# Half of the first tile's pairs among fields 0 to 15 taken ahead in two steps of 32 samples, and the first store held

## The chip, the core and the metric

The kernel runs on one core of a Trainium2 chip. TensorE does matmuls (its weight loads are rows of their own, PEld), VectorE (DVE) elementwise work and reductions, ScalarE (ACT) activations and copies, GpSimd (POOL) issues the indirect gathers, SyncE (SP) the other DMA transfers. The time is that of one execution on the device in microseconds, the median of several runs.

## What is computed

A recommender tower for 1024 samples, 33 fields and vectors of 128 numbers. The reference, cut to what matters:

```python
e = stack([tbl_f[ids[:, f]] for f in range(33)], axis=1)      # (1024, 33, 128)
row, col = np.triu_indices(33, k=1)                            # 528 pairs
inner = e[:, row] * e[:, col]
fm = relu(einsum('bpd,ad->bpa', inner, attn_W) + attn_b)
scores = einsum('ba,bpa->bp', gnn_feature, fm)
attn = softmax(scores, axis=1)
attn_output = einsum('bp,bpd->bd', attn, inner) * 100.0
z = concatenate([gnn_feature, attn_output, gnn_feature], axis=1)
h = relu(z @ W_top1 + b_top1); h = relu(h @ W_top2 + b_top2)
y = h @ W_top3
```

## The kernel before

**Tiles and steps.** The samples go in T = 8 tiles of 128. A tile has STEPS = 32 steps of GROUPS = 4 samples, so there are ALL = 256 steps S. The 528 pairs of a sample are laid out as K = 16 distances by F = 33 fields: pair (f, f + k) modulo 33 with k = 1 to 16. To read them without a modulus, x is held transposed in `xt` (128 rows for the vector's numbers, then sample, then 33 fields and fields 0 to 15 once more, written by `repeat`). A step has COLS = 4 x 528 = 2112 columns.

**One step.** VectorE multiplies (`product`, L418) into one of 4 buffers of `products`. ScalarE rounds most columns to the faster fp32r type (`round_inner`, L316, `inner_hi`), VectorE subtracts to get the rest (`rest_of_inner`, L423, `low_parts`). TensorE's `hidden` (L571) takes the columns in 5 chunks of 416 or 424: a *native* chunk is one fp32 matmul (L580, two records in the profile), a *split* chunk three fp32r matmuls (L587, L588, L589). `NATIVE[S]` says how many chunks are native: 4 and 3 in steps 0 and 1, 2 in six steps of a tile, 1 in the others. Two chunks share a buffer of the PSUM ring of 3; ScalarE's `relu` (L308) empties a buffer into `fm` (3 buffers). After hidden(S) of an even step, `reduce_steps(S - 2)` (L610) makes the scores of two steps: each step has 8 matmuls of 264 columns, whose 32 weight columns come from `gnn_blocks` at a place of their own for each group of samples j, and which write 32 rows of PSUM each (rows 32j on), so that the four j use different quarters of the array.

**Around the steps.** TensorE also transposes x (`transpose_x`, L620, eight fields at a time, into the ring; ScalarE's `evacuate_xt`, L347, copies them to `xt`), at steps 18, 20, 22, 24 and 26 for the next tile, and does `fields` (L634) and `mlp` for the tile before. Softmax parts stand at the first steps of a tile. `units` lists everything that takes a buffer of the ring, in the order in which TensorE claims them.

**The first tile.** GpSimd gathers 33 fields into `x_rows`, one indirect transfer a field (L280). TensorE transposes all five groups of fields as they land, then starts hidden(0). VectorE's product(0) waits for all five groups and the repeated fields.

**Queues.** Every engine runs its list in order. SyncE: loads of inputs, then `store_rows(0)` (the 128 x 33 rows of `x_rows` to `x_dram`, L230, when all fields are gathered), `store_rows(1)`, then the loads of `x_fields` from `x_dram` (L219) for the first tile. GpSimd's gather of tile 1 waits for the first store (it overwrites `x_rows`) and, group by group, for the transposes of tile 0. Gather 2 waits for the second store in the same way.

Of the kernel before, what the change touches and what calls it, by code (L numbers as in the profile page):

```python
# [7 lines left out]
ALU = mybir.AluOpType  # L8
# [4 lines left out]
def afm_tower(nc, gnn, ids, tables, w1, b1, w2, b2, w3, attn_w, attn_b, out):  # L13
    P = 128
    B, D = gnn.shape
    F = len(tables)
# [13 lines left out]
    assert EDGES[0][-1] == EDGES[1][-1] == COLS and ALL % 2 == 0  # L30
    H1, H2 = w1.shape[1], w2.shape[1]
# [13 lines left out]
    NATIVE[0], NATIVE[1] = 4, 3  # L45
    FIRST = 0
    SPLIT = COLS - min(EDGES[S % 2][NATIVE[S]] for S in range(ALL))
# [4 lines left out]
    XT_AT = (18, 20, 22, 24, 26)  # L52
    MLP_AT = (19, 21, 23)
    MAX_AT, EXP_AT, INV_AT, SCALE_AT, TURN_AT = 1, 2, 2, 3, 4
# [10 lines left out]
    def jobs_of(S):  # L65
# [4 lines left out]
        if s in XT_AT and t + 1 < T:  # L70
            jobs.append(("x_t", t + 1, XT_AT.index(s)))
# [7 lines left out]
    units = [("x_t", 0, c) for c in range(XJ)]  # L79
    for S in range(ALL):  # L80
        pair, odd = divmod(S, 2)
        units += [("hidden", pair, j) for j in ((3, 4) if odd else (0, 1, 2))] + jobs_of(S)
# [4 lines left out]
    with ctx:  # L87
# [96 lines left out]
        def taken_out(unit):  # L184

            kind, a, b = unit
            if kind == "hidden":
                return s_fm, SLOTS * a + b + 1
# [13 lines left out]
        def native_cols(S):  # L202
            return EDGES[S % 2][NATIVE[S]]

        def chunk_place(S, c):

            pair, odd = divmod(S, 2)
            j, h = divmod(CHUNKS * odd + c, 2)
            return slot(("hidden", pair, j)), h
# [4 lines left out]
        def _(sp):  # L214
# [26 lines left out]
            sp.dma_start(b2_sb[:], b2.rearrange("(m p) -> p m", p=P), allow_slow_non_contiguous=True).then_inc(s_weights, 16)  # L241
            store_rows(0)
# [52 lines left out]
        def _(act):  # L295
            def relu(pair, j):
                act.wait_ge(s_hidden, 2 * (SLOTS * pair + j + 1))
                S = 2 * pair
                if j == 0 and S >= FM_BUFS:
                    act.wait_ge(s_red, (S - FM_BUFS) // 2 + 1)  # L300
                if j == 2 and S + 1 >= FM_BUFS:
                    act.wait_ge(s_red, (S + 1 - FM_BUFS) // 2 + 1)
                n = THIN if j == 2 else WIDE
                at = [(S + c // CHUNKS) % FM_BUFS * COLS + EDGES[c // CHUNKS][c % CHUNKS] for c in (2 * j, 2 * j + 1)]
                first = fm[:, 0, 0:1]
                dst = bass.AP(tensor=first.tensor, offset=first.offset + at[0],
                              ap=[first.ap[0], [at[1] - at[0], 2], [1, n]])
                nc.scalar.activation(dst, slot(("hidden", pair, j))[:, :, 0:n], ACT.Relu,  # L308
                                     bias=attn_b_sb[:, 0:1]).then_inc(s_fm, 1)

            def round_inner(S):
                act.wait_ge(s_inner, S + 1)
                if S >= HI_BUFS:
                    act.wait_ge(s_hidden, CHUNKS * (S - HI_BUFS + 1))
                at = native_cols(S)
                nc.scalar.copy(inner_hi[:, S % HI_BUFS, 0:COLS - at], plain[:, S % INNER_BUFS, at:]).then_inc(s_hi, 1)  # L316
# [52 lines left out]
            for c in range(XJ):  # L369
                evacuate_xt(0, c)  # L370
                if c < K // FU:
                    repeat(0, c)
            round_inner(0)
            round_inner(1)
            for S in range(ALL):
                t, s = divmod(S, STEPS)
                relu(S // 2, 2 if S % 2 else 0)
                if part_at(S, EXP_AT) is not None:
                    exps(part_at(S, EXP_AT))
                if S + 2 < ALL:  # L380
# [3 lines left out]
                relu(S // 2, 3 if S % 2 else 1)  # L384
                if S % 2:
                    relu(S // 2, 4)
# [5 lines left out]
                if t + 1 < T and s - 1 in XT_AT[0:K // FU]:  # L392
# [13 lines left out]
        def _(dve):  # L406
            def product(S):
                if S >= INNER_BUFS:
                    dve.wait_ge(s_hidden, CHUNKS * (S - INNER_BUFS + 1))
                t, s = divmod(S, STEPS)  # L410
# [311 lines left out]
```

## Time and profile before

| | us |
|---|---|
| median of 3 runs | 1270.39 (1270.38 to 1270.89) |
| the profiled execution | 1270.63 |
| its span, first to last instruction | 1268.2 |
| TensorE busy | 1201.0 (95%) |
| VectorE busy | 1147.9 (91%) |
| ScalarE busy | 1018.7 (80%) |
| GpSimd busy | 451.8 (36%) |

The profile lists instructions with their start and duration, groups them by line and shape, names for an engine's idle time the releaser of the instruction that ended it, and gives the work of each engine in any stretch. Two instructions of an engine can overlap a little, so the distance of two starts is a better price than a duration. Matmul ends are modelled; a matmul's real cost is the distance to the next one's start. A row with "x8" is eight instructions in a row with their summed time.

### The profile page before, as it was taken

What the parts mean: (1) busy time and instruction counts of PE and PEld (TensorE: products, weight loads), DVE (VectorE), ACT (ScalarE), POOL (GpSimd) and SP (SyncE); (2) the same over time, 40 slices, a digit from 0 to 9 for tenths busy, and PEclk for the clock granted to TensorE, in tenths of its full rate; (3) what the DMA queues carried; (4) which work ended last, traced back from release to release, by engine and by line L of the source; (5) the groups of instructions that cost most, each with busy time, mean ns of one, the idle gap of its engine ahead of it and who ended that gap; (6) DMA issues with size and microseconds to landing.
All of it is one profiled execution on the core that took longest, in us unless ns stands there. A gap on an engine that the chain in (4) does not pass through costs nothing.

```text
span 1268.2 us, 20736 instructions
## 1 busy us (share of the span) xinstructions
PE 1201.0 (95%) x8732; PEld 898.7 (71%) x8732; DVE 1147.9 (91%) x649; ACT 1018.7 (80%) x1039; POOL 451.8 (36%) x270
## 2 busy tenths in 40 slices
PE   1499999999999999999999999999999999999998
PEld 1267676777777777777777777677777777777766
DVE  2399899998999989999899989999799998999994
ACT  1288898778987889878897798978888788887883
POOL 6587684018800386005840088201880000000000
PEclk9999999999999999999999999999999999999999
DMA  4211410311103111131101311031110300011001
GB/s 108 97 34 50 105 32 26 102 45 30 34 13 125 31 32 28 30 106 37 32 20 47 106 27 32 20 111 39 30 34 21 117 18 1 1 29 39 17 9 38
DMA packets 54859, 58.83 MB, mean 46 GB/s; under 512 B 10728, under 2 KB 49136, under 8 KB 53744
## 3 DMA queue, kind: packets, MB, share of 16 engines
q1 hardware_dynamic: 46304, 40.20, 10.4%
q0 software_dynamic: 8448, 17.32, 5.2%
q8 instruction: 69, 1.13, 0.4%
q14 instruction: 22, 0.18, 0.0%
q10 hardware_dynamic: 16, 0.00, 0.0%
HBM read 36.12 MB, written 17.31 MB: 42 GB/s over the span
## 4 chain that ended last, share of the span: by engine, by line
PE 83%; ACT 8%; issue 4%; DVE 2%; POOL 2%; another core or an unknown queue 1%; DMA 1%; SPq 0%; ACTq 0%; DVEq 0%; POOLq 0%
PE scores L610 19%; PE ring L580 17%; PE ring L587 13%; PE ring L589 12%; PE ring L588 12%; PE ring L634 4%; ACT fm L308 3%; ACT inner_hi L316 3%; PE ring L620 2%; POOL x_rows L280 2%; PE ring L654 1%; DVE products L418 1%; ACT exp_pairs L323 1%; PE ring L648 1%
## 5 line engine op out<-in xcount | busy, mean ns | idle before, releaser
L308 ACT ACTIVATE fm<-ring,attn_b_sb 128x848 f32<-128x848 f32 (+1 forms) x640 | 597.2, 971 | 183.1 <-PE ring L580 174.3
L418 DVE TENSOR_TENSOR products<-xt 128x2112 f32<-128x2112 f32 x256 | 601.9, 2351 | 37.1 <-ACT xt L347 37.1
L280 POOL DMA_INDIRECT x_rows<-in_tbl,ids_all x264 | 451.1, 1709 | 498.2 <-PE ring L620 408.3
L423 DVE TENSOR_TENSOR low_parts<-products,inner_hi 128x1688 fp32r<-128x1688 f32 (+4 forms) x256 | 467.1, 1825 | 57.1 <-ACT inner_hi L316 56.0
L587 PE MATMUL ring<-inner_hi,attn_wt_lo 128*128 128x424 f32 (+1 forms) x971 | 433.1, 446 | 5.1 <-ACT fm L308 5.1
L316 ACT CAST inner_hi<-products 128x1688 fp32r<-128x1688 f32 (+4 forms) x256 | 392.3, 1532 | 5.2 <-DVE products L418 5.2
L589 PE MATMUL ring<-inner_hi,attn_wt_hi 128*128 128x424 f32 (+1 forms) x971 | 344.1, 354 | 0.0
L588 PE MATMUL ring<-low_parts,attn_wt_hi 128*128 128x424 f32 (+1 forms) x971 | 343.7, 354 | 0.0
L580 PE MATMUL ring<-products,attn_wt 128*128 128x424 f32 (+1 forms) x618 | 275.8, 542 | 10.0 <-issue 6.4
L610 PE MATMUL scores<-fm,gnn_blocks 128*32 128x264 f32 x4096 | 254.6, 389 | 6.5 <-ACT exp_pairs L323 6.4
L587 PEld LDWEIGHTS ring<-inner_hi,attn_wt_lo 128*128 128x128 f32 x971 | 182.6, 188 | 70.8 <-issue 37.6
L588 PEld LDWEIGHTS ring<-low_parts,attn_wt_hi 128*128 128x128 f32 x971 | 183.0, 188 | 43.5 <-issue 40.1
L610 PEld LDWEIGHTS scores<-fm,gnn_blocks 128*32 128x32 f32 x4096 | 120.0, 109 | 107.7 <-issue 13.8
L589 PEld LDWEIGHTS ring<-inner_hi,attn_wt_hi 128*128 128x128 f32 x971 | 182.4, 188 | 5.2
L580 PEld LDWEIGHTS ring<-products,attn_wt 128*128 128x128 f32 x618 | 104.6, 190 | 85.4 <-issue 78.2
L620 PE MATMUL ring<-ident,x_rows 128*128 128x128 f32 x264 | 39.2, 292 | 34.0 <-DMA x_rows<-in_tbl,ids_all 31.1
L634 PE MATMUL ring<-attn_t,x_fields 128*128 128x128 f32 x512 | 62.5, 275 | 2.0 <-ACT attn_t L401 1.4
L634 PEld LDWEIGHTS ring<-attn_t,x_fields 128*128 128x128 f32 x512 | 61.8, 191 | 3.2 <-issue 3.1
L347 ACT COPY xt<-ring 128x1024 f32<-128x1024 f32 (+1 forms) x40 | 38.5, 964 | 31.3 <-PE ring L620 15.7
L620 PEld LDWEIGHTS ring<-ident,x_rows 128*128 128x128 f32 x264 | 33.0, 151 | 39.4 <-DMA x_rows<-in_tbl,ids_all 25.7
L473 DVE TENSOR_TENSOR attn<-ring,xt 128x1024 f32<-128x1024 f32 x30 | 36.6, 1220 | 2.8 <-PE ring L634 2.8
L481 DVE TENSOR_REDUCE pooled<-attn 128x32 f32<-128x1024 f32 x30 | 36.5, 1216 | 0.1
(53 smaller groups left out, 203.9 us busy)
## 6 DMA issues: line engine op xcount, KB each, us to landing
x_dram<-x_rows SPq DMA_DIRECT2D x8, 2112.0 KB, 6.6
x_fields<-x_dram SPq DMA_DIRECT2D x128, 128.0 KB
x_rows<-in_tbl,ids_all POOLq DMA_INDIRECT x264
attn_t<-attn_turned SPq DMA_DIRECT2D x124, 32.0 KB, 1.9
w_sb<-in_W_top SPq DMA_DIRECT2D x2, 512.0 KB
x_fields<-in_r_gnn_feature SPq DMA_DIRECT2D x1, 512.0 KB
h<-in_W_top SPq DMA_DIRECT2D x1, 256.0 KB
ids_all<-in_ids SPq DMA_DIRECT2D x1, 132.0 KB, 2.7
```

Of the source, the lines that this page charges most:

```text
L280: nc.gpsimd.indirect_dma_start(out=x_rows[:, f, :], out_offset=None, in_=tables[f], in_offset=bass.IndirectOffsetOnAxis(ap=ids_all[:, t, f ...
L308: nc.scalar.activation(dst, slot(("hidden", pair, j))[:, :, 0:n], ACT.Relu, bias=attn_b_sb[:, 0:1]).then_inc(s_fm, 1)
L316: nc.scalar.copy(inner_hi[:, S % HI_BUFS, 0:COLS - at], plain[:, S % INNER_BUFS, at:]).then_inc(s_hi, 1)
L418: nc.vector.tensor_tensor(dst, a, b, ALU.mult).then_inc(s_inner, 1)
L423: nc.vector.tensor_tensor(inner[:, S % INNER_BUFS, at:end], plain[:, S % INNER_BUFS, at:end], inner_hi[:, S % HI_BUFS, 0:end - at].bitcast ...
L580: nc.tensor.matmul(dst, attn_wt[:], plain[:, S % INNER_BUFS, begin:end], start=True, stop=True)\
L587: nc.tensor.matmul(dst, attn_wt_lo[:], hi, start=True, stop=False)
L588: nc.tensor.matmul(dst, attn_wt_hi[:], lo, start=False, stop=False)
L589: nc.tensor.matmul(dst, attn_wt_hi[:], hi, start=False, stop=True).then_inc(s_hidden, 1)
L610: last = nc.tensor.matmul(scores[I * j:I * j + I, h, 0:HALF], block_of(s, j), fm[:, S % FM_BUFS, at:at + HALF], start=s == 0, stop=s == ST ...
L620: last = nc.tensor.transpose(to[:, n // 4, n % 4 * P:(n % 4 + 1) * P], x_rows[:, FU * c + n, :], ident[:])
L634: last = nc.tensor.matmul(bank[:, h, to:to + QS * I], x[:, n, :], own[:, :, n, :], start=True, stop=True)
```

## The change

1. **Two steps ahead.** Steps S = -2 and -1 are added. Each takes 32 samples and the pairs (f, f + k) with f = 0 to 7 and k = 1 to 8, which need fields 0 to 15 alone: 64 pairs a sample, 2048 columns a step, 4 chunks of 512, all native. They stand after the first two transposes; the transposes of groups 2, 3 and 4 follow them.
2. **Short steps.** Steps 0 to 15 (the same 64 samples) have 464 pairs left a sample: 1856 columns, 4 chunks of 464. `product` makes them in two instructions (distances 1 to 8 with fields 8 to 32, and distances 9 to 16 with all fields). NATIVE[0], NATIVE[1] become 3, 2.
3. **Scores.** `reduce_steps(-2)`, after hidden(0), makes the scores of the samples ahead: 64 matmuls of 64 columns, each writing 8 runs of 8 columns in the scores' 33-column rows. In the short steps the first half of a sample's scores has 200 columns (8 runs of 25) instead of 264.
4. **The first store** waits until hidden(1) is done (QUIET = 2), and with it all that stands behind it on SyncE.
5. Chunks are numbered through the program and paired in that order (`CHUNK_LIST`, `PAIR_OF`), so a relu of a short step has 2 x 464 columns, of a step ahead 2 x 512. The two `repeat` copies of the first tile come after the relus of the steps ahead.

```diff
+    AHEAD, AHEAD_SAMPLES = 8, 32
+    BEGIN = -2
+    SHORT = -BEGIN * AHEAD_SAMPLES // GROUPS
-    NATIVE[0], NATIVE[1] = 4, 3
+    NATIVE[0], NATIVE[1] = 3, 2
...
+    def edges(S):
+        if S < 0:
+            return list(range(0, AHEAD_SAMPLES * AHEAD_PAIRS + 1, 512))
+        if S < SHORT:
+            return list(range(0, LEFT + 1, LEFT // 4))
+        return EDGES[S % 2]
...
+        if S == -1:
+            jobs += [("x_t", 0, c) for c in range(2, XJ)]
...
+            sp.wait_ge(s_hidden, hidden_by(QUIET - 1))
             store_rows(0)
             store_rows(1)
...
+                if S < 0:
+                    pieces = [((S - BEGIN) * AHEAD_SAMPLES, AHEAD_SAMPLES, 0, AHEAD, 1, AHEAD)]
+                elif S < SHORT:
+                    pieces = [(GROUPS * S, GROUPS, AHEAD, F - AHEAD, 1, AHEAD), (GROUPS * S, GROUPS, 0, F, AHEAD + 1, K - AHEAD)]
+                else:
+                    pieces = [(GROUPS * (S % STEPS), GROUPS, 0, F, 1, K)]
...
+            dve.wait_ge(s_xt_out, 2)
+            product(-2)
+            product(-1)
             dve.wait_ge(s_xt_out, XJ)
             dve.wait_ge(s_repeat, K // FU)
             product(0)
...
+                if S < 0:
+                    for i in range(AHEAD_SAMPLES):
+                        step, j = divmod((S - BEGIN) * AHEAD_SAMPLES + i, GROUPS)
+                        columns = fm[:, S % FM_BUFS, i * AHEAD_PAIRS:(i + 1) * AHEAD_PAIRS]
+                        yield step, j, step == 0, near[j][:, :, 0:AHEAD], columns.rearrange("p (k f) -> p k f", f=AHEAD)
+                    return
...
+                        if S < SHORT and h == 0:
+                            columns = fm[:, S % FM_BUFS, j * NEAR:(j + 1) * NEAR]
+                            yield s, j, False, near[j][:, :, AHEAD:F], columns.rearrange("p (k f) -> p k f", f=F - AHEAD)
+                            continue
...
-            for c in range(XJ):
+            for c in range(2):
                 transpose_x(0, c)
             pe.wait_ge(s_zero, 3)
-            for S in range(ALL):
+            for S in range(BEGIN, ALL):
                 hidden(S)
...
-                if S >= 2 and S % 2 == 0:
+                if S >= BEGIN + 2 and S % 2 == 0:
                     reduce_steps(S - 2)
```

**TensorE at the start, before.** L620 are the transposes (33 fields), L580 a native chunk, L587 to L589 a split one.

```order
3 L620 MATMUL ring<-ident,x_rows 128x128 x33
4 L580 MATMUL ring<-products,attn_wt 128x424 x4
5 L587 MATMUL ring<-inner_hi,attn_wt_lo 128x416
6 L588 MATMUL ring<-low_parts,attn_wt_hi 128x416
7 L589 MATMUL ring<-inner_hi,attn_wt_hi 128x416
8 L580 MATMUL ring<-products,attn_wt 128x416
```

**TensorE at the start, now.** The same lines are L682, L627 and L634 to L636; L673 are scores.

```order
3 L682 MATMUL ring<-ident,x_rows 128x128 x16
4 L627 MATMUL ring<-products,attn_wt 128x512 x8
5 L682 MATMUL ring<-ident,x_rows 128x128 x17
6 L627 MATMUL ring<-products,attn_wt 128x464 x3
7 L634 MATMUL ring<-inner_hi,attn_wt_lo 128x464
8 L635 MATMUL ring<-low_parts,attn_wt_hi 128x464
9 L636 MATMUL ring<-inner_hi,attn_wt_hi 128x464
10 L673 MATMUL scores<-fm,gnn_blocks 32x8x8 x64
11 L627 MATMUL ring<-products,attn_wt 128x464 x2
```

Eight chunks of 512 stand between the transposes of 16 and of 17 fields, and 64 matmuls of scores between hidden(0) and hidden(1).

**VectorE, the first products and subtractions, before** (L418 and L423).

```order
10 L418 TENSOR_TENSOR products<-xt 128x2112 x2
11 L423 TENSOR_TENSOR low_parts<-products,inner_hi 128x416
12 L418 TENSOR_TENSOR products<-xt 128x2112
13 L423 TENSOR_TENSOR low_parts<-products,inner_hi 128x848
14 L418 TENSOR_TENSOR products<-xt 128x2112
15 L423 TENSOR_TENSOR low_parts<-products,inner_hi 128x1264
```

**VectorE at the same place, now** (L464 and L470).

```order
10 L464 TENSOR_TENSOR products<-xt 128x2048 x2
11 L464 TENSOR_TENSOR products<-xt 128x800
12 L464 TENSOR_TENSOR products<-xt 128x1056
13 L464 TENSOR_TENSOR products<-xt 128x800
14 L464 TENSOR_TENSOR products<-xt 128x1056
15 L470 TENSOR_TENSOR low_parts<-products,inner_hi 128x464
16 L464 TENSOR_TENSOR products<-xt 128x800
17 L464 TENSOR_TENSOR products<-xt 128x1056
18 L470 TENSOR_TENSOR low_parts<-products,inner_hi 128x928
```

Two products of 2048 columns come first, and each later product is now two instructions with 1856 columns in all.

## Rows read from the trace of the kernel before

**Rows 1.** The page, part 1: busy us, share of the span, instructions.

```profile
PE 1201.0 (95%) x8732; PEld 898.7 (71%) x8732; DVE 1147.9 (91%) x649; ACT 1018.7 (80%) x1039; POOL 451.8 (36%) x270
```

**Rows 2.** Stretches, columns as the first line says, busy in us.

```profile
core 0: us, PE busy (x) PEld busy (x) DVE busy (x) ACT busy (x) POOL busy (x), PEclk, DMA share, GB/s
15.00:46.00 31.00, 5.88 (x24) 4.70 (x24) 0.23 (x2) 5.49 (x5) 23.43 (x25) 1.00 0.20 52
46.00:54.70 8.70, 2.18 (x9) 1.78 (x9) 2.41 (x2) 1.37 (x3) 0.07 (x1) 1.00 0.62 256
...
60.30:133.20 72.90, 72.56 (x502) 52.62 (x501) 72.61 (x38) 64.23 (x64) 53.34 (x32) 1.00 0.22 65
203.00:353.00 150.00, 147.96 (x1089) 111.02 (x1088) 142.18 (x82) 126.87 (x130) 64.10 (x35) 1.00 0.17 48
```

**Rows 3.** Timeline of the head: start us, us, engine, line, instructions, [idle before].

```profile
35.99 1.97 PE L620 MATMUL ring<-ident,x_rows 128*128 128x128 f32 x8 [7.95 <-DMA x_rows<-in_tbl,ids_all]
46.19 2.18 PE L620 MATMUL ring<-ident,x_rows 128*128 128x128 f32 x9 [8.22 <-DMA x_rows<-in_tbl,ids_all]
...
47.43 0.34 SPq L230 DMA_DIRECT2D x_dram<-x_rows  x1
...
38.00 1.08 ACT L347 COPY xt<-ring 128x1024 f32<-128x1024 f32 x1 [7.68 <-PE ring L620]
50.91 1.35 ACT L347 COPY xt<-ring 128x1024 f32<-128x1024 f32 x2 [11.83 <-remote]
...
52.29 4.63 DVE L418 TENSOR_TENSOR products<-xt 128x2112 f32<-128x2112 f32 x2 [37.07 <-ACT xt L347]
...
54.75 1.75 PE L580 MATMUL ring<-products,attn_wt 128*128 128x424 f32 x2 [6.38 <-issue]
```

**Rows 4.** The chain of waits in plain steps, TensorE: start us, us.

```profile
65.93 0.19 PE ring L588
...
67.46 1.92 PE scores L610 x32
...
72.59 0.71 PE ring L580 x2
```

**Rows 5.** Timeline of VectorE from 56 us.

```profile
56.84 0.58 DVE L423 TENSOR_TENSOR low_parts<-products,inner_hi 128x416 fp32r<-128x416 f32 x1
57.34 2.35 DVE L418 TENSOR_TENSOR products<-xt 128x2112 f32<-128x2112 f32 x1
...
66.48 1.92 DVE L423 TENSOR_TENSOR low_parts<-products,inner_hi 128x1696 fp32r<-128x1696 f32 x1
```

**Rows 6.** Timeline at the clock's rise, weight loads and a matmul row.

```profile
58.42 0.33 PEld L580 LDWEIGHTS ring<-products,attn_wt 128*128 128x128 f32 x1 [0.37 <-issue]
59.00 0.19 PEld L580 LDWEIGHTS ring<-products,attn_wt 128*128 128x128 f32 x1 [0.25 <-issue]
...
60.28 1.22 PE L580 MATMUL ring<-products,attn_wt 128*128 128x416 f32 x3
```

**Rows 7.** L610 alone in 0.03 us, columns as in rows 2.

```profile
67.41:67.44 0.03, 0.03 (x4) 0.03 (x8) 1.00 0.00 0
```

**Rows 8.** The page, part 5, weight loads of the scores.

```profile
L610 PEld LDWEIGHTS scores<-fm,gnn_blocks 128*32 128x32 f32 x4096 | 120.0, 109 | 107.7 <-issue 13.8
```

**Rows 9.** Timelines of GpSimd, SyncE and TensorE around the second gather.

```profile
54.63 3.11 POOL L280 DMA_INDIRECT x_rows<-in_tbl,ids_all  x1 [8.88 <-DMA x_dram<-x_rows]
...
124.70 0.33 SPq L230 DMA_DIRECT2D x_dram<-x_rows  x1
...
133.20 1.03 PE L620 MATMUL ring<-ident,x_rows 128*128 128x128 f32 x8
...
153.81 1.06 PE L620 MATMUL ring<-ident,x_rows 128*128 128x128 f32 x8 [0.76 <-ACT fm L308]
...
172.20 0.27 PE L620 MATMUL ring<-ident,x_rows 128*128 128x128 f32 x1
```

**Rows 10.** Timeline of TensorE, fields of the first tile.

```profile
241.86 1.95 PE L634 MATMUL ring<-attn_t,x_fields 128*128 128x128 f32 x16
```

More of the change, by code:

```diff
@@ L76, in jobs_of, with hidden_by, relus_by, pairs_of_steps @@
         return jobs
-    units = [("x_t", 0, c) for c in range(XJ)]
-    for S in range(ALL):
-        pair, odd = divmod(S, 2)
-        units += [("hidden", pair, j) for j in ((3, 4) if odd else (0, 1, 2))] + jobs_of(S)
+    CHUNK_LIST = [(S, c) for S in range(BEGIN, ALL) for c in range(chunks(S))]
+    CHUNK_NO = {chunk: n for n, chunk in enumerate(CHUNK_LIST)}
+    PAIR_OF = [CHUNK_LIST[n:n + 2] for n in range(0, len(CHUNK_LIST), 2)]
+    def hidden_by(S):
+        return CHUNK_NO[S, chunks(S) - 1] + 1
+    def relus_by(S):
+        return CHUNK_NO[S, chunks(S) - 1] // 2 + 1
+    def pairs_of_steps(S):
+        return (S - BEGIN) // 2
+    units = [("x_t", 0, c) for c in range(2)]
+    for S in range(BEGIN, ALL):
+        units += [("hidden", n, 0) for n, pair in enumerate(PAIR_OF) if pair[0][0] == S] + jobs_of(S)
     units += [("fields", T - 1, c) for c in (2, 3)] + [("mlp", T - 1, n) for n in range(3)]
@@ L202, in native_cols @@
         def native_cols(S):
[L203 removed]
+            return edges(S)[NATIVE[S]] if S >= 0 else edges(S)[-1]
         def chunk_place(S, c):
[L207 to L209 removed]
+            return divmod(CHUNK_NO[S, c], 2)
         block = ctx.enter_context(nc.Block())
@@ L368, in _ @@
             nc.scalar.copy(attn_wt_hi[:], attn_wt[:]).then_inc(s_setup, 1)
-            for c in range(XJ):
+            for c in range(2):
                 evacuate_xt(0, c)
[L371 to L375, printed above, removed]
+            for S in range(BEGIN, ALL):
                 t, s = divmod(S, STEPS)
-                relu(S // 2, 2 if S % 2 else 0)
+                out_now = [n for n, pair in enumerate(PAIR_OF) if pair[1][0] == S]
+                relu(out_now[0])
                 if part_at(S, EXP_AT) is not None:
                     exps(part_at(S, EXP_AT))
-                if S + 2 < ALL:
+                if 2 <= S + 2 < ALL:
                     round_inner(S + 2)
@@ L383, in _ @@
                     scale_attn(part_at(S, SCALE_AT))
-                relu(S // 2, 3 if S % 2 else 1)
-                if S % 2:
-                    relu(S // 2, 4)
+                for n in out_now[1:]:
+                    relu(n)
+                if S in FIRST_REPEAT_AT:
+                    repeat(0, FIRST_REPEAT_AT[S])
                 for kind, of, c in jobs_of(S):
@@ L526, in _ @@
             product(0)
-            product(1)
-            rest_of_inner(0)
-            product(2)
-            for S in range(ALL):
+            for S in range(BEGIN, ALL):
                 t, s = divmod(S, STEPS)
-                if S + 1 < ALL:
+                if 0 <= S + 1 < ALL:
                     rest_of_inner(S + 1)
@@ L571, in hidden @@
             def hidden(S):
-                pe.wait_ge(s_inner, S + 1)
-                for c in range(CHUNKS):
-                    begin, end = EDGES[S % 2][c:c + 2]
-                    bank, h = chunk_place(S, c)
-                    dst = bank[:, h, 0:end - begin]
+                pe.wait_ge(s_inner, S - BEGIN + 1)
+                for c in range(chunks(S)):
+                    begin, end = edges(S)[c:c + 2]
+                    n, h = chunk_place(S, c)
+                    dst = slot(("hidden", n, 0))[:, h, 0:end - begin]
                     if h == 0:
-                        claim(("hidden", S // 2, (CHUNKS * (S % 2) + c) // 2))
-                    if c < NATIVE[S]:
+                        claim(("hidden", n, 0))
+                    if S < 0 or c < NATIVE[S]:
                         nc.tensor.matmul(dst, attn_wt[:], plain[:, S % INNER_BUFS, begin:end], start=True, stop=True)\
```

104 lines of the change are left out of this document (59 added, 45 removed).

## The prediction

> **What bounds the kernel now.** I read the busy shares first and then the table of stretches, which says where the busy share is not the whole story. TensorE is busy for 95% of the span [rows 1]. By stretches [rows 2] the kernel has a head of 54.7 us, in whose last two parts TensorE works 5.88 us of 31 and 2.18 of 8.7, and after it a body in which it is busy all the time: 72.56 of 72.90 us in the first 18 steps, 147.96 of 150 us in one later tile. So there are two ways to save: start the body earlier, or take matmul time out of the body. The change tries both: it does 4096 columns of hidden products in the head, where TensorE is idle.
>
> The head, in order of time [rows 3]: TensorE transposes the third group of eight fields at 35.99, as soon as its gather lands, and ScalarE copies it out at 38.00, 2.0 us later; the two groups before it stand in the same way. The fourth group is transposed at 46.19 and copied at 50.91, 4.72 us later, so 2.7 us behind the pattern, and the profile can only name "remote" for it. Meanwhile SyncE issued the 2 MB store of x_rows at 47.43, and the DMA engines moved 256 GB/s in that stretch against 52 before it [rows 2, 3]. Products follow at 52.29, hidden(0) at 54.75.
>
> In the body's first 18 steps VectorE is as full as TensorE: 72.61 of 72.90 us [rows 2]. Both would have to get faster, so both are summed below. TensorE's chain of waits in a plain step is a row of matmuls with no hole in it [rows 4].
>
> **Units, all at full clock.** In the chain a matmul of a split chunk of 424 columns takes 0.19 us, the three of a chunk 0.58; a native chunk is 0.71 us, in two records; the scores of two steps, 32 records, take 1.92 us [rows 4]. In columns: 464 native is 0.71 x 464/424 = 0.78, 464 split 0.63. VectorE: a subtraction of 416 columns takes 0.58 us, of 1696 columns 1.92, so 1.05 ns a column and 0.14 fixed, of which 0.08 overlaps the next instruction (56.84 + 0.58 against 57.34) [rows 5].
>
> **Start of the body.** If the held store is what delayed the fourth copy, the copy moves from 50.91 to 48.2: 2.7 us. The alternative is zero. I take 2.7, because the copies without a store beside them come after 2.0 us and nothing else is in flight there; it is one case, so a rival below. product(0) has 800 + 1056 columns in two instructions instead of 2112 in one: 0.90 + 1.17 = 2.07 against 2.27, 0.2 us less. hidden(0) thus begins at 54.75 - 2.9 = 51.85. The work taken ahead must be out of the way by 46.19: products of 2048 columns, 2.3 us each, from about 29.2, when the second group's copy ends (its row stands 9.9 us before the third's), eight chunks of 512 from 31.5. At half clock a chunk costs 1.71 us (1.41 for 424, since a record's weight load of 0.33 comes 0.37 after the one before [rows 6]), so 13.7 us and an end at 45.2 if the clock never rose; in this trace it rose about 4.1 us into steady work (54.75 to between 58.42 and 59.00, where the weight load of L580 goes from 0.33 to 0.19 us and the records from 0.70 to 0.35 apart, the levels of 1.2 and 2.4 GHz; the granted clock in the profile's column does not show it) [rows 3, 6]. Then they end near 40.5. Either way they cost nothing; neither do their four relus of some 1.2 us, hidden in the same hole of ScalarE (38.00 + 1.08 to 50.91).
>
> **hidden(0).** Before: 54.75 to 60.28, 5.5 us, of which 4.1 at half clock. After: three native chunks at 1.55 at half clock; 4.1 us cover 2.65 of them, the rest 0.27, the split chunk 0.63: 5.0. Saved 0.5.
>
> **Steps 1 to 18, hidden.** Before there are 26 native and 64 split chunks: 26 x 0.71 + 64 x 0.58 = 55.6 us. After, steps 1 to 15 have 21 native and 39 split chunks of 464 (40.9 us) and steps 16 to 18 are as before (9.2 us): 50.1. Saved 5.5. With eight pairs of scores (15.4) the sum of before is 71.0 of the 72.9 measured from 60.28 to 133.20 [rows 6, 9]; I leave that 1.9 as it is.
>
> **Scores of the short steps.** 32 records go in eight groups of four that run side by side (four matmuls are in the array at once in [rows 7]), 0.24 us a group. In half of the groups 264 columns become 200; if their time goes by columns, 0.058 us less each, 0.23 for a pair of steps, 1.9 for eight.
>
> **Scores of the samples taken ahead.** This is what the change adds to TensorE's full stretch: 64 matmuls of 64 columns, 128 records, between hidden(0) and hidden(1). Three prices. By columns alone a group of four is 0.24 x 64/264 = 0.058 us, 32 groups 1.9 us. By the weight load, which now lasts longer than the matmul that should cover it (109 ns [rows 8]), 32 x 0.109 = 3.5 us. By L610's own rate, 1.92 us for 32 records, 60 ns each, 7.7 us. I take 3.5: eight loads and four matmuls are under way within the same 0.03 us [rows 7], so records can follow each other far closer than 60 ns, and the load is the next thing that is longer than the columns. Both ends stay for the range.
>
> The Trainium skill speaks against me here. "TensorE: Matmul & The Clock Gate", section "Wait — 56ns, not 53.3ns?", says that without hardware decoding the sequencer spends about 62 ns on each matmul, which bounds short ones; 128 of them would be 7.9 us. The trace's 60 ns a record of L610 looks like that rule, but eight loads under way at once do not. The case is a rival, priced from L610's row.
>
> **Is TensorE still the bound?** VectorE's short step is 2.07 + 1.53 (1392 columns) = 3.6, or 3.1 where two chunks are native (928 columns). From 49.6 to the subtraction of step 18 it has 16 short products (33.1), 16 short subtractions (0.6 + 6 x 1.04 + 9 x 1.53 = 20.6), four long products (9.1) and three long subtractions (5.1), 68 us, so it is through near 117.5. TensorE's sum ends hidden(18) at 51.85 + 5.0 + 3.5 + 50.1 + 13.5 + 1.9 = 125.9 against 133.20. ScalarE was busy for 64.23 of the 72.90 us before, and its share of a step shrinks with the same columns. TensorE stays last.
>
> **The held store.** SyncE issues it when hidden(1) is done, 51.85 + 5.0 + 3.5 + 2.8 = 63.2 instead of 47.43. Behind it on SyncE's queue wait the second store and the loads of x_fields, and on GpSimd the whole second gather: its first row moves from 54.63 to 70.4, and the second store, which comes when its last has landed, from 124.70 to 140.5 [rows 9]. The transposes that need the gather come at 133.20 to 172.20, 7 us earlier after; the last group has 24 us left. So the delay costs nothing, but the second store, 7.2 us long like the first (47.43 to 54.63), now runs at 140.5 to 147.7, and the third group of transposes, which read x_rows, moves from 153.81 [rows 9] to 146.5: the edge of it.
>
> **Sum.** 2.7 + 0.2 + 0.5 + 5.5 + 1.9 - 3.5 = 7.3 us. Later steps are as before and shift as a whole. Against the profiled execution (1270.63 us, 1268.2 of it span) that is 1263.3; the median of the runs shown, 1270.39, is 0.2 below it, so I say **1263.1**.
>
> **Rivals.**
> - *The stall stays, or moves to the second store* (18%). For: "remote" names no cause, and the second store meets the transposes of the second tile at its edge. Against: the pattern of 2.0 us. 2.7 less gained: 1265.8.
> - *More than summed* (14%): the array is still at full clock when hidden(0) begins, since it worked from 31.5 on (half of 4.1, 2.05 us more), or the scores ahead cost 1.9. 1261.1 and 1261.5. Against the first: it stands idle from about 41.5 to 46.19 and 47.4 to 51.85.
> - *The short scores keep L610's rate* (10%): 7.7 instead of 3.5, 1267.3. The page's rule would come out there too.
> - *Other gains lost* (5%): the ring of three slots or ScalarE holds up the short steps, or the later steps' waits for relu take the lead back. About 1269.5.
> - *Slower* (3%): the short matmuls do not run four abreast, because each has its own weights and writes eight runs of eight columns. Nearest row: 1.95 us for 16 records of 128 columns that use the whole array [rows 10], 0.12 each, 15.6 us for 128. 12.1 more than I took: 1275.2. It turns slower from 10.8 us on, 84 ns a record.
> - The rest, 50%, is my forecast, within 1261.8 to 1264.5.
>
> That the change does not do what it says can be set aside: the order of instructions shows the eight chunks of 512 ahead of the last transposes.
>
> **Numbers.** Measurements of this kernel can tell about 0.2%, 2.5 us, from no change. Faster: 50 + 18 + 14 and half of the 10 at the limit, 87%. Within: the other half and the 5, 10%. Slower 3%. The range 1260.0 to 1267.6 leaves out some 2% below (both of the extra gains) and the last cases above.
>
> **What would show it.** The fourth copy out of x_t should begin near 48.2, hidden(0) near 51.9; L673, the new line of the scores, should show its first 128 records in 1.9 to 3.5 us (7.7 would be L610's rate, 15.6 the slower rival); the transposes of the second tile should begin at about 125.9, and every later stage 7 us earlier, with the later tile as long as before. Wrong would be: a "remote" wait that is still there, TensorE waiting for relu or for the subtractions in steps 1 to 15, or a stall at 140 to 150.

## The result, and the profile after

The changed kernel takes **1264.38 us** (median of 6 runs, 1263.74 to 1264.97); the kernel before, beside it on the same chip, 1270.6. The ratio is 0.995, with a 95% interval of 0.994 to 0.9961: faster by 6.2 us, half a per cent and clear of the noise, where 7.3 us were forecast. The profiled execution took 1263.74 us, its span 1261.6.

The total is close, but two of the terms behind it are wrong, and their errors cancel in part. The stretches of the new kernel, in the columns of [rows 2] (busy time and instructions of each engine, then TensorE's granted clock, DMA share, GB/s):

```profile
core 0: us, PE busy (x) PEld busy (x) DVE busy (x) ACT busy (x) POOL busy (x), PEclk, DMA share, GB/s
...
46.00:54.77 8.77, 2.18 (x9) 1.78 (x9) 2.21 (x3) 1.93 (x4) 1.83 (x2) 0.50 0.08 22
60.14:62.06 1.92, 1.92 (x129) 1.83 (x128) 1.92 (x3) 1.21 (x2) 0.00 (x0) 1.00 0.03 9
62.06:127.52 65.46, 65.46 (x463) 44.50 (x457) 62.49 (x48) 54.53 (x54) 46.54 (x27) 1.00 0.18 59
202.00:352.00 150.00, 147.97 (x1095) 111.00 (x1087) 142.17 (x80) 126.96 (x130) 75.57 (x43) 1.00 0.18 52
```

The third of these rows is the body's first part: 65.46 us from hidden(1) to the second tile's first transposes, where the kernel before had 72.92 (60.28 to 133.20) [rows 2, 6, 9]. That is 7.46 us less, and 7.4 were summed. The row ahead of it is what the scores of the samples taken ahead add: 1.92 us, not 3.5. A later stretch of 150 us is as full as before [rows 2].

The head is where the surprise is. The timeline of the new kernel's head (start us, us, engine, line, instructions, [idle before <- what ended it]):

```profile
28.44 0.94 POOL L320 DMA_INDIRECT x_rows<-in_tbl,ids_all  x1 [0.30 <-issue]
29.09 4.49 DVE L464 TENSOR_TENSOR products<-xt 128x2048 f32<-128x2048 f32 x2 [13.99 <-issue]
29.69 2.50 POOL L320 DMA_INDIRECT x_rows<-in_tbl,ids_all  x1 [0.31 <-issue]
32.50 1.90 POOL L320 DMA_INDIRECT x_rows<-in_tbl,ids_all  x1 [0.30 <-issue]
34.71 0.95 POOL L320 DMA_INDIRECT x_rows<-in_tbl,ids_all  x1 [0.31 <-issue]
...
40.36 1.04 PE L682 MATMUL ring<-ident,x_rows 128*128 128x128 f32 x8
...
45.48 1.08 ACT L386 COPY xt<-ring 128x1024 f32<-128x1024 f32 x1 [2.79 <-remote]
...
47.19 0.94 POOL L320 DMA_INDIRECT x_rows<-in_tbl,ids_all  x1 [0.31 <-issue]
48.42 2.18 PE L682 MATMUL ring<-ident,x_rows 128*128 128x128 f32 x9 [7.03 <-DMA x_rows<-in_tbl,ids_all]
51.17 1.35 ACT L386 COPY xt<-ring 128x1024 f32<-128x1024 f32 x2 [4.62 <-PE ring L682]
52.56 4.23 DVE L464 TENSOR_TENSOR products<-xt 128x800 f32<-128x800 f32 x4 [18.97 <-ACT xt L386]
```

Three things stand in it. The fourth copy begins 2.75 us after its transposes, not 4.72 as in [rows 3], so the 2.0 us were gained there. But a "remote" wait is still there, now ahead of the third copy (45.48, 5.1 us behind its transposes), where no store is in flight at all. And the transposes of the fourth group begin at 48.42 instead of 46.19 [rows 3]: two of GpSimd's gather rows took 2.50 and 1.90 us instead of 0.94, just while VectorE made the two products ahead. So product(0) starts at 52.56 against 52.29, hidden(0) at 54.77 against 54.75 [rows 3]: of the 2.9 us forecast for the start of the body nothing arrived.

A later row of the same view shows the scores ahead, 128 records of 64 columns:

```profile
60.14 1.99 PE L673 MATMUL scores<-fm,gnn_blocks 128*32 128x64 f32 x128
```

### The profile page after: what moved, and what is told of

It reads as the page before. It is cut to its first block, busy times and chain, and to the rows that moved or that the text cites. A ratio compares the mean times of both kernels' runs of the same rounds, so it can differ in the third digit from the quotient of the medians.

```text
span 1261.6 us, 20957 instructions
## 1 busy us (share of the span) xinstructions
PE 1203.4 (95%) x8830; PEld 895.1 (71%) x8830; DVE 1144.7 (91%) x667; ACT 1015.3 (80%) x1035; POOL 450.1 (36%) x270
## 4 chain that ended last, share of the span: by engine, by line
PE 85%; ACT 8%; issue 4%; POOL 3%; DVE 1%; DMA 0%; ACTq 0%; DVEq 0%; POOLq 0%
PE scores L673 20%; PE ring L627 18%; PE ring L634 13%; PE ring L636 12%; PE ring L635 12%; PE ring L696 4%; ACT fm L347 3%; POOL x_rows L320 3%; ACT inner_hi L355 2%; PE ring L682 2%; PE ring L716 1%; ACT exp_pairs L362 1%; PE ring L710 1%; PE ring L706 0%; ACT h L394 0%
## 5 line engine op out<-in xcount | busy, mean ns | idle before, releaser
L347 ACT ACTIVATE fm<-ring,attn_b_sb 128x848 f32<-128x848 f32 (+2 forms) x636 | 597.6, 976 | 192.4 <-PE ring L627 177.4
L464 DVE TENSOR_TENSOR products<-xt 128x2112 f32<-128x2112 f32 (+3 forms) x274 | 603.0, 2206 | 33.0 <-ACT xt L386 19.0
L470 DVE TENSOR_TENSOR low_parts<-products,inner_hi 128x1688 fp32r<-128x1688 f32 (+6 forms) x256 | 462.4, 1806 | 58.6 <-ACT inner_hi L355 57.7
L634 PE MATMUL ring<-inner_hi,attn_wt_lo 128*128 128x424 f32 (+2 forms) x957 | 430.2, 450 | 4.5 <-ACT fm L347 4.5
L355 ACT CAST inner_hi<-products 128x1688 fp32r<-128x1688 f32 (+6 forms) x256 | 388.6, 1518 | 3.9 <-DVE products L464 3.7
L636 PE MATMUL ring<-inner_hi,attn_wt_hi 128*128 128x424 f32 (+2 forms) x957 | 339.8, 355 | 0.0
L635 PE MATMUL ring<-low_parts,attn_wt_hi 128*128 128x424 f32 (+2 forms) x957 | 339.5, 355 | 0.0
L627 PE MATMUL ring<-products,attn_wt 128*128 128x424 f32 (+3 forms) x630 | 285.3, 550 | 11.4 <-DVE products L464 7.8
L673 PE MATMUL scores<-fm,gnn_blocks 128*32 128x264 f32 (+2 forms) x4224 | 255.0, 382 | 6.5 <-ACT exp_pairs L362 6.4
L634 PEld LDWEIGHTS ring<-inner_hi,attn_wt_lo 128*128 128x128 f32 x957 | 180.2, 188 | 70.5 <-issue 39.2
L673 PEld LDWEIGHTS scores<-fm,gnn_blocks 128*32 128x32 f32 x4224 | 121.8, 109 | 106.5 <-issue 15.7
L636 PEld LDWEIGHTS ring<-inner_hi,attn_wt_hi 128*128 128x128 f32 x957 | 179.8, 188 | 5.8
L627 PEld LDWEIGHTS ring<-products,attn_wt 128*128 128x128 f32 x630 | 107.4, 191 | 91.7 <-issue 79.0
L682 PE MATMUL ring<-ident,x_rows 128*128 128x128 f32 x264 | 38.2, 288 | 25.1 <-DMA x_rows<-in_tbl,ids_all 22.1
L682 PEld LDWEIGHTS ring<-ident,x_rows 128*128 128x128 f32 x264 | 32.3, 148 | 30.6 <-DMA x_rows<-in_tbl,ids_all 15.8
```

The source lines that it names most:

```text
L347: nc.scalar.activation(dst, slot(("hidden", n, 0))[:, :, 0:wide], ACT.Relu, bias=attn_b_sb[:, 0:1]).then_inc(s_fm, 1)
L355: nc.scalar.copy(inner_hi[:, S % HI_BUFS, 0:end - at], plain[:, S % INNER_BUFS, at:end]).then_inc(s_hi, 1)
L464: last = nc.vector.tensor_tensor(dst, a, b, ALU.mult)
L470: nc.vector.tensor_tensor(inner[:, S % INNER_BUFS, at:end], plain[:, S % INNER_BUFS, at:end], inner_hi[:, S % HI_BUFS, 0:end - at].bitcast ...
L627: nc.tensor.matmul(dst, attn_wt[:], plain[:, S % INNER_BUFS, begin:end], start=True, stop=True)\
L634: nc.tensor.matmul(dst, attn_wt_lo[:], hi, start=True, stop=False)
```

## Experiments

Three questions were open: what delays a copy by 2.7 us ("remote"), what lengthens the gather rows, and what the hold of the first store is worth or costs. The kernels ran in four groups, each on a chip of its own and beside the kernel before; on three of these chips that took 1267.0 to 1267.6 us, on one 1270.2, and in the result above 1270.6. This difference turns out to be part of the answer.

### Without the hold, and the hold alone

The changed kernel with its store issued at once:

```
-            sp.wait_ge(s_hidden, hidden_by(QUIET - 1))
             store_rows(0)
```

> The changed kernel with the first store issued as soon as the gather has landed (no hold). The changed kernel has hidden(0) at 54.77 us and its fourth copy 2.75 us after its transposes began at 48.42; the kernel before has 4.72 us between them. Theory A (the store beside the transposes is what delays the copy): the copy comes 4.7 us after the transposes again, hidden(0) near 56.7, median near 1266.3. Theory B (the delay has nothing to do with the store, as the third group's copy of the changed kernel, 5.1 us after its transposes with no store in flight, suggests): hidden(0) stays at 54.8 and the median at 1264.4.

The kernel before with the hold and nothing else:

```
+            sp.wait_ge(s_hidden, 2 * CHUNKS)
             store_rows(0)
```

> The kernel before with nothing but the first store held until hidden(1) is done. Theory A: the fourth copy comes 2.0 us after its transposes, near 48.2, hidden(0) near 52.0, median near 1267.9. Theory B: copy at 50.9, hidden(0) at 54.75, median 1270.6.

Without the hold: 1262.86 us, ratio 0.9966 (0.9953 to 0.9978). The copy follows its transposes after 2.01 us although the store is issued between the two:

```profile
48.53 2.18 PE L681 MATMUL ring<-ident,x_rows 128*128 128x128 f32 x9 [6.94 <-DMA x_rows<-in_tbl,ids_all]
...
49.79 0.34 SPq L269 DMA_DIRECT2D x_dram<-x_rows  x1
50.54 1.35 ACT L385 COPY xt<-ring 128x1024 f32<-128x1024 f32 x2 [6.67 <-PE ring L681]
```

So a store beside it is not enough to delay the copy. On this chip the kernel before has no delay either (1267.18 us); whether the hold takes the delay away on a chip that has it is answered by the run with a pause, below.

The hold alone: 1285.04 us, ratio 1.0141 (1.0124 to 1.0157), 18 us *slower*. GpSimd's timeline:

```profile
68.90 42.93 POOL L281 DMA_INDIRECT x_rows<-in_tbl,ids_all  x1 [23.29 <-DMA x_dram<-x_rows]
112.14 1.57 POOL L281 DMA_INDIRECT x_rows<-in_tbl,ids_all  x1 [0.30 <-issue]
```

And VectorE's, whose rows follow each other from 60 to 127 us without a hole, each beginning up to 0.08 us before the last one ends (four of them stand here):

```profile
67.60 1.91 DVE L424 TENSOR_TENSOR low_parts<-products,inner_hi 128x1688 fp32r<-128x1688 f32 x1
69.43 2.35 DVE L419 TENSOR_TENSOR products<-xt 128x2112 f32<-128x2112 f32 x1
71.70 1.48 DVE L424 TENSOR_TENSOR low_parts<-products,inner_hi 128x1272 fp32r<-128x1272 f32 x1
73.10 2.35 DVE L419 TENSOR_TENSOR products<-xt 128x2112 f32<-128x2112 f32 x1
```

The gather starts at 68.90 here, 14.3 us later than in [rows 9]. One of its rows, 0.94 us when VectorE is idle, took 42.93 us. The last row of the second gather came at 174.9 us, and TensorE stood still for rows of x (its waits from 130 to 190 us: us in total, times, longest):

```profile
PE ring L621 <- DMA x_rows<-in_tbl,ids_all: 14.2, 2, 7.7
```

The prediction's "the delay costs nothing" counted 24 us of slack behind the gather and forgot that the gather itself runs on an engine that VectorE can shut out. In the changed kernel the first row at 73.05 got through in 1.26 us; there the hold was harmless by luck.

### Products ahead and the gather's rows

The kernel before with two VectorE products of the same 2048 columns, into a buffer that nobody reads:

```
+            dve.wait_ge(s_xt_out, 2)
+            for d in range(2):
...
+                nc.vector.tensor_tensor(dst, a, b, ALU.mult)
```

> The kernel before with two more VectorE products of 2048 columns at 29.1 us, whose results nobody reads (added work, result otherwise the same). In the changed kernel two gather rows of GpSimd at 29.69 and 32.50 took 2.50 and 1.90 us instead of 0.94, beside just those products, and the fourth group's transposes came at 48.42 instead of 46.19. Theory G (VectorE's products hold up GpSimd's issue of the gather): the same two rows are long here, the fourth transposes begin near 48.4, hidden(0) 2.2 us later than before, near 57.0. Theory H (something else of the change, as TensorE's matmuls or the relus, delays the gather): rows of 0.94 throughout and 46.2.

One run, 1269.47 us, 2.3 us above the kernel before on that chip (1267.18). The same two rows are long, and only they:

```profile
29.04 4.49 DVE L531 TENSOR_TENSOR products<-xt 128x2048 f32<-128x2048 f32 x2 [14.30 <-ACT xt L347]
29.67 2.47 POOL L280 DMA_INDIRECT x_rows<-in_tbl,ids_all  x1 [0.30 <-issue]
32.45 1.90 POOL L280 DMA_INDIRECT x_rows<-in_tbl,ids_all  x1 [0.30 <-issue]
34.66 0.94 POOL L280 DMA_INDIRECT x_rows<-in_tbl,ids_all  x1 [0.31 <-issue]
```

All 33 rows are a chain in which each takes 0.94 us and 0.30 to issue, so what one loses all later ones lose: the fourth transposes came at 48.39, against 45.92 in the run with the hold alone on the same chip, whose head is that of the kernel before. The hidden products ahead have no part in that.

Then the cure. Half of the products' input is also in PSUM, where TensorE's transposes left it; the changed kernel with the first operand read from there:

```
+                    if S < 0:
+                        a = slot(("x_t", 0, 0))[:, 0, sample:sample + samples]
+                        a = bass.AP(tensor=a.tensor, offset=a.offset, ap=[a.ap[0], a.ap[1], [0, distances], [P, fields]])
```

TensorE also has to leave that buffer alone until both products are made, so its next claim of it waits for them:

```
+                if n == 0:
+                    pe.wait_ge(s_inner, 2)
```

> The changed kernel, but the two products ahead read their first operand (fields 0 to 7) from the PSUM buffer into which they were transposed, so VectorE has one operand in SBUF instead of two. Theory G1 (GpSimd is held up by VectorE reading two operands from SBUF): the gather rows stay at 0.94 us, the fourth transposes begin near 46.2, hidden(0) near 52.5, median near 1262.2. Theory G2 (any VectorE work that writes or reads SBUF holds GpSimd up): the two gather rows are long as before, transposes at 48.4, median 1264.4.

**1259.88 us**, ratio 0.9941 (0.9924 to 0.9958), better than both kernels. The products take the same 4.49 us, and the rows beside them 0.94:

```profile
28.96 4.49 DVE L467 TENSOR_TENSOR products<-ring,xt 128x2048 f32<-128x2048 f32 x2 [14.07 <-ACT xt L386]
29.62 0.94 POOL L320 DMA_INDIRECT x_rows<-in_tbl,ids_all  x1 [0.30 <-issue]
30.87 0.94 POOL L320 DMA_INDIRECT x_rows<-in_tbl,ids_all  x1 [0.30 <-issue]
...
45.84 1.86 PE L687 MATMUL ring<-ident,x_rows 128*128 128x128 f32 x9 [4.19 <-DMA x_rows<-in_tbl,ids_all]
```

It is thus not VectorE's work as such but its second operand in SBUF. The Trainium skill says so too: "SBUF — State Buffer", section "SBUF: two separate sides", has VectorE and GpSimd share a pair of ports as an exclusive lock, which a VectorE operation with two SBUF inputs takes, though only against a GpSimd operation that reads SBUF. The trace agrees, 2.50 us against 0.94, if the gather's issue reads SBUF (its offsets, `ids_all`, lie there). The page has the other engine blocked for the length of one instruction; the 42.93 us beside VectorE instructions of at most 2.35 us go beyond that, and the measurement decides.

### Both kernels again on another chip

> The changed kernel again, beside the kernel before on the same chip. If the delay of the copy ('remote') belongs to a chip or a run and not to the kernel, the gain over before is 4.0 to 4.5 us here (3.4 of the first result's 6.2 less what the copies' delays of 2.7 and 0.8 us make: 6.2 - 1.9 = 4.3). If it belongs to the kernel before alone, the gain is 6.2 again.

> The kernel before again, for its trace on this chip. Its profile showed the fourth copy 4.72 us after its transposes; the executions of before in the first call were 3.4 us shorter than the first ones. If the delay belongs to a chip or a run: copy 2.0 us after the transposes (48.2), hidden(0) near 52.0, span near 1265.5. If to the kernel: 50.9, 54.75 and 1268.2.

The changed kernel took 1263.03 us, 0.9967 (0.9955 to 0.998) of the kernel before, which took 1267.03 there (9 runs) and 1267.22 in the run of its trace. In the kernel before, unchanged, the store is issued 1.4 us after the transposes and the copy still follows at 2.0 us:

```profile
45.78 2.18 PE L620 MATMUL ring<-ident,x_rows 128*128 128x128 f32 x9 [8.04 <-DMA x_rows<-in_tbl,ids_all]
...
47.16 0.34 SPq L230 DMA_DIRECT2D x_dram<-x_rows  x1
47.78 1.35 ACT L347 COPY xt<-ring 128x1024 f32<-128x1024 f32 x2 [8.93 <-PE ring L620]
```

So the 2.7 us that I read in [rows 3] are no property of the kernel; they go with the chip of that trace (or the hour of its runs, which no run here separates). The change itself is worth 4.0 us here, against 6.2 on the first chip, and 2.0 of the difference is the delay that its fourth copy escaped there. The body's first part gives less here too: 72.33 us (57.72 to 130.05) became 65.46 (62.29 to 127.75), 6.9 saved and not 7.46.

### Fillers to keep the clock up, with and without the hold

In the PSUM version the array stands idle for 4.2 us ahead of the fourth transposes, and hidden(0) runs at half clock for most of its time; in the changed kernel it did so for its first 4.4 us, where 4.1 were forecast. To the PSUM version 9 matmuls that nobody reads were added behind the third transposes and 8 behind the last:

```
+                        if (S, c) == (-1, 2):
+                            fill(("x_t", 0, 3), 9)
+                        if (S, c) == (-1, XJ - 1):
+                            fill(("hidden", 4, 0), 8)
```

> e4_psum with 9 idle-time matmuls of 264 columns between the third and the fourth group's transposes and 8 between the fifth group's and hidden(0), on constant inputs into free ring buffers (added work, result the same). In e4_psum the clock falls at 46.22 and rises at 56.45, and hidden(0) from 51.12 runs mostly at 1.2 GHz. Theory C (the idle time is what costs hidden(0) its clock): the clock stays at 2.4 GHz, hidden(0) takes 3.0 instead of 5.4 us, median 2 us under e4_psum, if VectorE then keeps up. Theory D (VectorE's products and subtractions pace the first steps anyway): less than 0.7 us.

> e4_psum without the hold of the first store. On the chip of the first call the copy came 2.0 us after the fourth transposes with the store beside it (e1_nohold, e3_dummy). Theory B (the store does not delay the copy, so the hold gains nothing): same as e4_psum within 0.5 us. Theory A: 2 us slower.

The fillers did what they should in the head: TensorE's weight loads stay at 0.19 us or less from 36.8 us on, the level of 2.4 GHz (the granted clock reads 1.00), hidden(0) took 3.25 us (51.22 to 54.47) instead of 5.77, and x_t(1,0), the second tile's first transposes, began at 121.87 us instead of 124.28. But the time was 1259.90, the same. Most of the gain went to the gather, which the hold had start where VectorE has no hole:

```profile
66.72 16.54 POOL L320 DMA_INDIRECT x_rows<-in_tbl,ids_all  x1 [20.86 <-DMA x_dram<-x_rows]
...
152.88 1.09 PE L687 MATMUL ring<-ident,x_rows 128*128 128x128 f32 x8 [1.36 <-DMA x_rows<-in_tbl,ids_all]
```

From the third transposes (142.15) to the fourth it is 10.73 us, in the new kernel 9.20 (147.80 to 157.00). Without the hold and without fillers: 1259.93 us, ratio 0.9946 (0.9929 to 0.9962), so the hold gains nothing here either. That version ran on the same chip as the one with fillers and shows where the lead goes: 2.05 us at x_t(1,0) (123.92 to 121.87), 0.45 at x_t(1,4) (162.57 to 162.12), 0.13 at the last transposes (1031.94 to 1031.82). Of the last 0.3 us the cause is open.

### A pause of VectorE under the hold

The hold alone, with VectorE waiting ahead of product(6):

```
+                    if S + 3 == 6:
+                        dve.wait_ge(s_hidden, CHUNKS * 5)
```

> The kernel before with its first store held until hidden(1) is done, as in the run that held the store alone, and one more edit: VectorE waits ahead of product(6) until TensorE has done five hidden stages, a pause of a microsecond or two near 72 to 75 us. Theory 1, GpSimd's first row of gather(1) cannot get through beside an unbroken row of VectorE instructions: that row took 42.93 us there; it should now end right behind the pause, so at 73 to 76 us, after 5 to 8 us, gather(1)'s last row should be near 140 us instead of 174.9, TensorE should no longer wait for gathered rows at x_t(1,1) to x_t(1,4), and the time should be 1267 to 1271 us against 1285.0 with the hold alone. Theory 2, the row is long for another reason (the store or the rows in memory that it reads): the pause changes nothing, the row still takes some 40 us and the time stays near 1285 us.

1272.28 us, ratio 1.0015 (1.0006 to 1.0025), on the chip where the kernel before takes 1270.19: of 18 us lost 2 are left, no more than the pause itself can cost, which was 3.4 us. The first three rows of the gather lie in it at 0.94 us each, and TensorE waited for no gathered row any more (VectorE's timeline, then GpSimd's):

```profile
69.81 1.91 DVE L424 TENSOR_TENSOR low_parts<-products,inner_hi 128x1688 fp32r<-128x1688 f32 x1
75.15 2.36 DVE L419 TENSOR_TENSOR products<-xt 128x2112 f32<-128x2112 f32 x1 [3.43 <-PE ring L592]
```

```profile
71.70 0.94 POOL L281 DMA_INDIRECT x_rows<-in_tbl,ids_all  x1 [26.21 <-DMA x_dram<-x_rows]
72.94 0.95 POOL L281 DMA_INDIRECT x_rows<-in_tbl,ids_all  x1 [0.30 <-issue]
74.19 0.94 POOL L281 DMA_INDIRECT x_rows<-in_tbl,ids_all  x1 [0.30 <-issue]
75.44 2.88 POOL L281 DMA_INDIRECT x_rows<-in_tbl,ids_all  x1 [0.30 <-issue]
```

This confirms that the loss of the hold alone was the starved row.

The same trace answers the question of the copy. Its chip has the delay, its store is held to 63.84 us, and the fourth copy still begins 4.32 us after its transposes:

```profile
45.81 2.18 PE L623 MATMUL ring<-ident,x_rows 128*128 128x128 f32 x9 [8.02 <-DMA x_rows<-in_tbl,ids_all]
50.13 1.35 ACT L348 COPY xt<-ring 128x1024 f32<-128x1024 f32 x2 [10.85 <-remote]
63.84 0.34 SPq L230 DMA_DIRECT2D x_dram<-x_rows  x1
```

With the store it was 4.72 [rows 3]. So the hold does not take the delay away, and the step of the prediction on which the 2.7 us rested falls.

### PSUM, fillers, no hold: twice

The version with fillers, without the hold:

```
-            sp.wait_ge(s_hidden, hidden_by(QUIET - 1))
```

> The changed kernel with the first operand of the two products ahead read from PSUM and the 17 filler matmuls, as in the run that had both (1259.90 us), and without the hold of the first store. There x_t(1,0) began at 121.87 us, 2.4 us earlier than without the fillers (124.28), but gather(1)'s first row took 16.54 us and TensorE then waited 1.5 us for gathered rows. Theory 1, that start of gather(1) beside a gapless VectorE ate the gain: without the hold gather(1) is issued from about 54.6 us on, where VectorE still waits for TensorE between products, its first row takes under 4 us, its last is issued near 122 us, x_t(1,0) stays near 121.9 us and the whole takes 1257.5 to 1258.3 us, 2 us under the 1259.9 of the version with PSUM alone. Theory 2, the gain of the fillers is given back elsewhere whatever the gather does (VectorE is the bound of the first steps): 1259.5 to 1260.2 us.

It took 1270.11 us, where the kernel before took 1270.19 on that chip: ratio 0.9996 (0.9987 to 1.0005). Both expectations missed by ten microseconds. The trace shows one long wait, of the kind of [rows 3]:

```profile
40.83 1.07 PE L686 MATMUL ring<-ident,x_rows 128*128 128x128 f32 x8
...
50.07 2.12 ACT L346 ACTIVATE fm<-ring,attn_b_sb 128x1024 f32<-128x1024 f32 x2 [8.36 <-remote]
51.23 6.71 PE L736 MATMUL ring<-w_sb,attn_wt 128*128 128x264 f32 x18 [9.34 <-ACT fm L346]
...
57.78 1.15 PE L686 MATMUL ring<-ident,x_rows 128*128 128x128 f32 x9
```

TensorE had done the work by 41.9 us; ScalarE, idle, went on at 50.07. The fillers then made it worse: they need the buffer that ScalarE frees, so the nine of them (18 records) stand from 51.23 on ahead of the fourth transposes, at half clock at first (granted 0.50 from 48 to 55 us), and take 6.55 us that they would have spent in an idle stretch. So the same kernel ran again on another chip, with its partner without fillers:

> The same kernel as the one that took 1270.11 us (products ahead from PSUM, 17 filler matmuls, no hold), once more. In that run the time was lost in one place: x_t(0,2)'s transposes ended at 41.9 us, and ScalarE started on what waits for TensorE there only at 50.07 us, after 8.4 us of idle time with no work of this kernel in between; x_t(0,3)'s transposes came at 57.78 us instead of 46.15. Theory 1, TensorE's signals arrive late on some chips (the kernel before took 1270.2 and 1270.6 us there, and 1267.0 and 1267.2 us on the two where its fourth copy followed its transposes after 2.0 us), and the kernel itself is not at fault: on a chip where before takes about 1267 us this kernel takes 1257.5 to 1258.3 us, x_t(0,3) is at about 46.2 us and x_t(1,0) at about 121.9 us. Theory 2, the fillers or the early store make that wait whatever the chip: the time is again within 1 us of before's, and x_t(0,3)'s transposes are again behind 55 us.

> The version with PSUM and without the hold and the fillers (1259.93 us before, where the kernel before took 1267.03), as the partner of the run above on the same chip. Theory 1, a chip with prompt signals: 1259.9 us again, 2 us above the version with fillers. If the kernel before takes about 1270 us on this chip, signals are late here too, and this version should then lose 2 to 9 us as well, without any filler; under theory 2 it should stay 7 us below before on any chip, since it has no fillers.

1259.71 us (5 runs), ratio 0.9938 (0.9925 to 0.9952), and 1260.45 us, 0.9945 (0.9931 to 0.9958); before took 1267.64. The fourth transposes were at 45.71, with the same fillers and the same early store. So the kernel alone does not cause the wait, which again goes with the chip; but of the 12.1 us by which the fourth transposes were late (45.71 to 57.78) more than half are the fillers' behind it. The version without fillers was not run on such a chip. But the 1257.5 to 1258.3 us expected did not come either: the two versions cannot be told apart. With the fillers VectorE's first wait comes at 82 us, without them at 61.67, so the gather starves without the hold too:

```profile
56.61 26.07 POOL L319 DMA_INDIRECT x_rows<-in_tbl,ids_all  x1 [11.22 <-DMA x_dram<-x_rows]
...
152.37 1.09 PE L686 MATMUL ring<-ident,x_rows 128*128 128x128 f32 x8 [1.45 <-DMA x_rows<-in_tbl,ids_all]
```

With the hold the row began at 66.72 and ended at 83.26, without it at 56.61 and 82.68: ten microseconds apart at the start, half a one at the end. It ends at a place in VectorE's row, 0.65 us behind the start of the first instruction that had to wait, and VectorE's row is the same in both but for the 0.6 us. Without the hold:

```profile
82.03 1.61 DVE L472 TENSOR_TENSOR low_parts<-products,inner_hi 128x1392 fp32r<-128x1392 f32 x1 [0.17 <-ACT inner_hi L354]
```

With it:

```profile
82.60 1.61 DVE L473 TENSOR_TENSOR low_parts<-products,inner_hi 128x1392 fp32r<-128x1392 f32 x1 [0.16 <-ACT inner_hi L355]
```

In the partner without fillers the first row took 7.91 us, from 54.33 to 62.24, and VectorE's first wait, of 0.25 us, ended at 61.67.

## Why the prediction was right, and where it was not

- **Fourth copy after 2.0 us, body 2.7 us earlier: wrong.** The failed step is "If the held store is what delayed the fourth copy", with "nothing else is in flight there" as its ground. The copy comes after 2.0 us beside a store (1262.86 us run, and the kernel before on the other chip), it comes after 4.32 us without one on a chip with the delay (hold with the pause), and a "remote" wait came ahead of the third copy where no store was. In the first trace the delay did shrink, by 1.97 us (4.72 to 2.75), but nothing shows that it was because of the hold; that it shrank is luck. The rival "the stall stays, or moves" (18%) had named it, although to another place.
- **"Either way they cost nothing" (the work taken ahead): wrong.** I looked for the engines that do the work, and for ScalarE's hole, and not for who shares a port with VectorE. Two gather rows lost 2.50 - 0.94 + 1.90 - 0.94 = 2.5 us, and the fourth transposes came 2.2 us later (46.19 to 48.42). With product(0) shorter by 0.25 (0.2 were forecast), the start of the body is 2.2 - 2.0 - 0.25 = 0.0 instead of -2.9.
- **hidden(0), 5.0 us: 5.37** (54.77 to 60.14), 0.16 saved and not 0.5. The clock did rise 4.4 us in (59.2 us), after it had fallen again at 45.6.
- **Hidden products of steps 1 to 18 and the short steps' scores, 5.5 + 1.9: right**, 7.46 measured from hidden(1) on, 6.9 on the other chip.
- **Scores ahead, 3.5 us: 1.92.** The term was mis-sized; the bound "by columns alone", 1.9, was right. Neither the weight load (109 ns) nor a cost for each record bounds them: the 128 records take 15 ns each (30 for each of the 64 matmuls), so the 62 ns that the prediction quotes from "TensorE: Matmul & The Clock Gate" of the Trainium skill, section "Wait — 56ns, not 53.3ns?", do not show here, and the rival that rested on L610's rate falls.
- **"So the delay costs nothing": wrong as reasoning.** The gather did have the slack, and the transposes at 137.65 and 147.80 show no stall; but a held gather may meet a VectorE without holes, and then it costs 18 us (hold alone) or 1.4 (fillers).
- **The sum.** To x_t(1,0) it is 0.0 - 0.16 + 1.92 - 7.46 = -5.7 us (133.20 to 127.52), and 6.0 at the third tile's (280.23 to 274.22). The span is 6.6 shorter; the last 0.7 us come in the last tile, where TensorE in the kernel before waits 0.54 us at 1233.90 for a DMA into `attn_t` and in the changed one does not. The forecast has no such term. The forecast had 2.9 us too many at the start, 0.3 too many in hidden(0) and priced the scores 1.6 too dear: 1264.38 lies well within 1260.0 to 1267.6, by terms that cancel in part, and 2.0 us of the gain are the delay that shrank by luck. On chips without the delay the change is worth 4.0 us.

## What to carry to other kernels

Before work is put into an engine's idle time, ask which engine shares its ports: two fp32 operands in SBUF on VectorE hold up a gather that GpSimd issues, and one operand in PSUM does not. A GpSimd gather should start where VectorE still waits now and then; the better balanced and the more gapless the loop is, the more a late start costs. And a stall that one trace shows and for which the profile names no work should be looked for in a second chip's trace before any of its time is counted as a gain.

## What the runs showed of the hardware

- **A gather row can starve for tens of microseconds.** The first row of the second gather took 0.94 to 3.11 us in ten traces and 7.91, 16.54, 26.07 and 42.93 us in four, these beside a VectorE without holes; three of the four ended 0.57 to 0.66 us after VectorE's first wait, of 0.16 to 0.25 us, was over, and the fourth ended at 111.83 without one. Most later rows pass in 1 to 2.5 us each between the same instructions. Open is why the first ones at 73.05 (changed kernel) and 54.63 (PSUM, no hold) passed in 1.26 and 1.41 us, where VectorE had no wait either.
- **ScalarE goes on late after TensorE, on some chips.** A "remote" wait of ScalarE (11.8, 2.8, 10.8 and 8.4 us long; 2.3 to 8.4 us of it too long) stands in all four traces from chips on which the kernel before takes 1270 us, and in none of the ten from the three chips where it takes 1267. What causes it stays open, also whether TensorE's signal or ScalarE itself is late; the store is excluded, since the wait also comes without one (2.3 us too long in the kernel before with its store held).
- **Small matmuls pack well.** 128 records with 64 columns and 128 x 32 weights of their own took 1.92 us, 15 ns each, which is what their columns cost at the price of L610's records (0.24 us for four of 264 columns).
